# Eight unused full-array matmuls per row, and a burst of 18, in the polynomial attention of an audio tower on one core

## What is computed

```python
qn = _normalize(q) * (scale * temperature)          # 8 heads of 8 channels
kn = _normalize(k) * scale
vN = concatenate([ones, v], -1) / N                 # N = 188
kv_mod = einsum('bhni,bhnj,bhne->bhije', kn, kn, vN)
kv     = einsum('bhnd,bhne->bhde', kn, vN)
y = A * einsum('bhni,bhnj,bhije->bhne', qn, qn, kv_mod) \
    + scale**2 * Bc * einsum('bhnd,bhde->bhne', qn, kv) + scale**4 * Cc * vsum
out = (y[..., 1:] / y[..., :1]) @ Wproj.T + bproj
```

## Time and profile before

| | |
|---|---|
| median of 3 runs | 1999.03 us (1997.1 to 2000.07) |
| profiled execution | 2006.71 us, of which span 2004.9 us |
| mean granted clock of TensorE | 0.865 |
| TensorE (PE) busy | 1719.6 us, 86% of the span, 15064 matmuls |
| VectorE (DVE) busy | 1488.5 us, 74% |
| ScalarE (ACT) busy | 756.6 us, 38% |
| GpSimd (POOL) busy | 690.5 us, 34% |

### The profile page before, as it was taken

How to read it: one execution, slowest core, us unless ns; L and a number is a source line. 1 busy time by engine, 2 the same in 40 slices (tenths; PEclk the granted TensorE clock), 3 DMA queues, 4 the chain that set the end, 5 groups by cost and what they waited for, 6 DMA issues and landing times. The chain is left out here.

```text
span 2004.9 us, 45616 instructions
## 1 busy us (share of the span) xinstructions
PE 1719.6 (86%) x15064; PEld 1344.4 (67%) x15064; DVE 1488.5 (74%) x4423; ACT 756.6 (38%) x2274; POOL 690.5 (34%) x957
## 2 busy tenths in 40 slices
PE   1499999999769999999999999973999999788887
PEld 1266666666557777777777777752888888677776
DVE  6166676666627898888889888875766665688887
ACT  2245454545324444344344444321222222343442
POOL 2622222222134555545545445532211111322221
PEclk9999999999869999999999999985555555788788
DMA  2000000000000000000000000000000000000000
GB/s 114 1 2 0 0 0 0 0 0 0 1 1 1 1 2 0 0 0 0 0 0 0 0 0 0 1 1 0 1 0 0 0 0 1 1 5 8 4 6 11
DMA packets 6980, 8.13 MB, mean 4 GB/s; under 512 B 6272, under 2 KB 6272, under 8 KB 6784
## 3 DMA queue, kind: packets, MB, share of 16 engines
q1 hardware_dynamic: 6912, 7.25, 1.1%
HBM read 5.71 MB, written 1.54 MB: 4 GB/s over the span
## 5 line engine op out<-in xcount | busy, mean ns | idle before, releaser
L1142 ACT ACTIVATE ex_pT<-ex_T 128x376 f32<-128x376 f32 (+1 forms) x384 | 162.8, 440 | 217.1 <-PE ex_T L1044 207.9
L604 ACT ACTIVATE al_prob<-al_S,al_negmax 94x94 f32<-94x94 f32 (+1 forms) x512 | 146.2, 375 | 180.0 <-DVE al_negmax L731 180.0
L1207 DVE TENSOR_REDUCE ex_negmax<-ex_R 94x2 bf16<-94x376 f32 (+1 forms) x384 | 186.8, 543 | 30.6 <-PE ex_R L1015 30.0
L1044 PE MATMUL ex_T<-ex_qm,ex_kpad 128*128 128x188 f32 x1024 | 189.7, 329 | 0.0
L505 PE MATMUL al_S<-al_kpad,al_qT 128*94 128x376 f32 x384 | 166.5, 516 | 0.0
L1044 PEld LDWEIGHTS ex_T<-ex_qm,ex_kpad 128*128 128x128 f32 x1024 | 163.0, 192 | 5.1
L944 POOL TENSOR_SCALAR_AFFINE_SELECT ex_pT<-ex_pT 128x512 f32<-128x512 f32 x128 | 84.3, 659 | 236.5 <-ACT ex_pT L1142 236.5
L682 POOL TENSOR_TENSOR al_kpad<-al_kT,al_quad_mask 128x1504 f32<-128x1504 f32 x32 | 86.2, 2692 | 186.3 <-ACTq L619 186.3
L731 DVE TENSOR_REDUCE al_negmax<-al_S 94x2 f32<-94x376 f32 (+1 forms) x192 | 99.1, 542 | 62.6 <-PE al_S L506 56.7
L1554 POOL TENSOR_TENSOR ta_kk<-ta_ext 94x320 f32<-94x320 f32 x64 | 60.4, 961 | 246.4 <-DVE ta_qkn L1734 163.0
L1027 PE MATMUL ex_R<-ex_sxT,wsb 128*128 128x188 f32 x256 | 72.3, 364 | 47.5 <-DVE ex_negmax L1207 47.5
(11 more groups left out here) (308 smaller groups left out, 4300.8 us busy)
## 6 DMA issues: line engine op xcount, KB each, us to landing
tok_xin<-x_t SPq DMA_DIRECT2D x4, 760.0 KB, 6.9
wsb<-weights SPq DMA_DIRECT2D x1, 2531.0 KB, 14.2
out<-stream SPq DMA_DIRECT2D x16, 94.0 KB
tok_par<-tok_w SPq DMA_DIRECT2D x1, 4.5 KB, 1.7
```

The lines of the kernel that those rows point to most:

```text
L604: last = nc.scalar.activation(p[:, k, cols], S[0:P, k, cols], ACT.Exp, bias=negmax[g % 2][:, m:m + 1])
L1044: last = nc.tensor.matmul(T[:, k, (j % 2) * N:(j % 2 + 1) * N], kpad[par][:, j, 0:K0], qm[e % 2][:], start=True, stop=True)
L1142: nc.scalar.activation(pT[e % 2][rows, k, cols], T[rows, k, cols], ACT.Exp)\
L1207: red(dst, src, AX.X, ALU.max, negate=True).then_inc(sem["r_used"], 1)
```

## The change

TensorE gets a helper that issues matmuls whose results nobody reads: 128 rows by 128 columns of weights from `w_parts`, 512 columns of data from `w_parts`, bf16, into the bank that the next step overwrites. Per turn in which its step is valid it issues three ahead of `QQ`, one ahead of `KV`, one ahead of `Y`, two ahead of `QKV` and one ahead of `XT`, each behind that step's waits. In turn 7, before the first `OUT` transpose, it issues 18 more. One of the two `sem_inc(settled)` goes. Nothing else changes, and the other engines get the same instructions as before.

```diff
-    ident, ones = env["ident"], env["ones"]
+    ident, ones, w_parts = env["ident"], env["ones"], env["w_parts"]
+    WARM = 18
...
+            def keep_busy(bank, n):
+
+                for _ in range(n):
+                    nc.tensor.matmul(bank, w_parts[:, 0, 0:128], w_parts[:, 0, 128:640], start=True, stop=True)
+
             def body(t, par):
                 r = t - 7
+                if isinstance(r, int) and r == 0:
+                    keep_busy(OUT[:], WARM)
...
                     need(pe, qqT_ready, 3 * r)
+                    for bank in (QQ0, QQ1, QT):
+                        keep_busy(bank[:], 1)
...
                     need(pe, kv_ready, 3 * r)
-
+                    keep_busy(KV[:], 1)
...
                     need(pe, y_ready, r)
+                    keep_busy(Y[:], 1)
...
                     need(pe, qkv_ready, r)
+                    keep_busy(QKV[:], 2)
...
                     need(pe, xT_ready, r)
-                    pe.sem_inc(settled, 1)
+                    keep_busy(XT[:], 1)
```

## The result

The changed kernel takes 2006.59 us (median of 9 runs, 1999.37 to 2012.97), the kernel before 1999.03 (median of 9). The ratio is 1.0037 with a 95% interval of 1.0022 to 1.0052: slower by 7.6 us, where 47 were forecast. One execution of the kernel before, of 4323 us, that fell in the first round of experiments counts as slow and is in none of the ratios. The profiled execution took 2011.12 us, with a span of 2009.2. In the two profiled executions the layer, from its first matmul to the start of its last lot of them, went from 320.6 us (1391.90 to 1712.49) to 332.9 (1387.57 to 1720.51), so by 12.3 us. The other layers, which were not changed, came out 8 us shorter in that execution: the layer's first matmul starts 4.3 us earlier, and 3.7 us less follow behind it.

What follows compares the result with a forecast made beforehand. The prediction took TensorE at half clock to bound the attention layer. Fixed costs of 21 us plus 25.6 us over 27 full turns gave +47, less 7.7 from the profiled 2006.7: 2046 us, range 1964 to 2082.

Steps and rivals of the forecast that it cites:

- the likeliest case: Full-clock share between 0.1 and 0.35 in the 27 full turns, 2015 to 2070 us; chance 0.55.
- the break-even case: Full-clock share from 0.41 to 0.47 in the full turns, time within 4 us of 1999; chance 0.05.
- What bounds the layer: Polynomial attention: TensorE at half clock, 9.85 us a turn; VectorE's floor 7.2 us, full-clock turns 7.2 to 7.5.
- Price of an unused matmul: Each 512-column unused matmul takes 0.43 us at the half clock, 0.21 us at the full one.
- The start: Turns 1 to 6 and the burst of 18 before the full turns: +9.6 and +6.4 us.
- f = 0.2: Share of PE's working time at full clock in the 27 full turns; 10.8 us a turn, +25.6 us.
- the mixture's 0.7: Full-clock share in the mixture layer, from its mean clock of 0.85; taken as a case between the bounds.
- The formula 12.35/(1 + f) + 0.5: Length in us of a full turn with full-clock share f, not under 7.2; break-even 9.07 us at f = 0.44.
- The end: Turns 34 to 37 carry 16 unused matmuls, 6.8 us at low clock, 3.4 at full; taken as 5 us.
- The signs: Profile: 0.50 until the burst, then mean near 0.6, falls during `KV` and `Y`, rises near `QQ`; refuted above 0.72.
- Rival "the clock holds": Full clock through the layer, turns of 7.2 to 7.5 us, -50 us, 1949 us; chance 0.11.

Runs made afterwards that it cites:

- lean: As late, with one unused matmul ahead of `QKV` in place of two; 1933.6 us, ratio 0.9675 to the kernel before.
- late: As hold, but with no unused matmul ahead of turn 7 except the burst of 18; 1935.8 us, ratio 0.9699 to the kernel before.
- qq4: The changed kernel with four unused matmuls ahead of `QQ` in place of three; 1986.6 us, ratio 0.9936 to the kernel before.
- hold: The changed kernel plus unused matmuls before the `added` wait, in `KV`, and two between `Y` halves; one moved from `QQ` to `XT`; 1943.6 us.
- burst_only: The changed kernel without the eight unused matmuls per row, burst of 18 kept, second signal back; 1999.9 us, ratio 0.9996 to the kernel before.
- thin: The changed kernel with unused matmuls of 32 columns of weights in place of 128, same streamed columns; 2115.6 us, ratio 1.0578 to the kernel before.

## Why the prediction was wrong

The direction was right and the sum of +47 us was not. The wide range from 1964 to 2082 us holds the 2006.6, but the likeliest case with its own 2015 to 2070 us does not, and the measured share of full clock, 0.42, lies in the break-even case, which was given a chance of 0.05 (0.41 to 0.47) and a time within 4 us of 1999. The direction has some luck in it: more than half of the +47 was to come from the 27 turns, and these came out 1.6 us shorter; the layer is slower only by its start and its end. By the prediction's own steps:

- **What bounds the layer: right.** Half clock, PE-bound, 9.85 us a turn. At the full clock a turn is 7.41 us (lean) to 7.64 (late, with two unused matmuls in VectorE's chain), in the changed kernel 7.45, where 7.2 to 7.5 was given.
- **Price of an unused matmul: right.** 0.43 us at the half clock and 0.21 at the full one were taken; the rows have 1505.79 to 1506.22, 0.43, and 1489.32 to 1489.54, 0.22. A turn wholly at the half clock is 13.1 us, where 12.85 was the sum.
- **The start: mis-sized.** 9.6 + 6.4 = 16 us were taken. From the first `XT` to turn 7's `OUT` transpose it went from 25.6 us (1391.90 to 1417.46) to 33.3 (1387.57 to 1420.90), +7.8. The step assumed that the clock rises only in the burst; it rose in turn 6. So part of turn 6's own work ran at double speed, and the burst took 3.9 us (1417.01 to 1420.90), all of it at the full clock.
- **f = 0.2, "nearer to this layer's 0 than to the mixture's 0.7": this is the step that failed.** Measured, 0.42. It was to cost 25.6 us over 27 turns, and they came out at 264.3 us against 265.9, a gain of 1.6. The step behind it was "I expect the clock to fall there nearly every turn, and then to be short of dense work for most of a slow turn". The places of the rise and the fall were foreseen about right, how often they come was not. The same sparse stretch was passed at the full clock turn after turn, for 33 us on end, before the clock fell; and in four turns of each cycle the clock rose for a moment, so that such a turn took 10.1 us, a third of it at the full clock. A hold over several turns and a flicker in each turn were treated as rivals, and the kernel does both in alternation. The neighbours in the trace before, 0 and 0.7, did not determine where between them it would lie. What sets the length of the stretches stays open.
- **The formula 12.35/(1 + f) + 0.5: too kind.** With f = 0.42 it gives 9.2 us, measured 9.79. It credits full-clock time with PE's speed, while VectorE's 7.5 us caps it. Mixing by time the changed kernel's own turns, 13.1 us at the half clock and 7.45 at the full one, gives 1/(0.58/13.1 + 0.42/7.45) = 9.9 us, and for the break-even turn of 9.07 us a share of 0.59, where the formula had 0.44; qq4 has just these 9.07 us at 0.60. The two errors had opposite signs: by the formula f = 0.42 would have been worth 27 x (9.85 - 9.2) = 18 us of gain where 1.6 came, so the second error hid part of the first.
- **The end: right.** 5 us were taken; from turn 34's `OUT` transpose to the last it took 34.4 us (1685.21 to 1719.61) against 28.3, +6.2.
- **The signs:** the rise near `KV`, behind the `QQ` lot, was as foreseen, and the falls that are shown lie just behind `KV` and `Y`, ahead of `QKV`. "0.50 until the burst" was wrong (it rose in turn 6), the mean clock of the full turns is 0.71 and not near 0.6, which is just short of the 0.72 that was to refute the forecast, and the turns are 9.8 us on the mean, not 10 to 11.
- **Rival "the clock holds":** not what this kernel does, but reachable: 1943.6 us in hold, where 1949 was given. Its argument against was a fall behind sparse work; with more filling there, and more in sum, the falls were gone.

The layer's +12.3 us is so 7.8 - 1.6 + 6.2, but for rounding. That the medians differ by 7.6 and not by 12 us is within what one execution differs from another (1999 to 2013 us for the changed kernel); what gave some of it back in the other layers was not followed up.

## What to carry to other kernels

Where the granted clock is at half in a stretch in which TensorE is busy, ask what fills the array: 95% busy with narrow fp32 matmuls held nothing here. Unused full-width matmuls can buy the clock if there are enough of them. The readings here suggest a dense lot to raise it and filling in the sparsest stretch so that it never falls, but the kernels that held the clock also had 1.3 to 1.4 times the changed kernel's unused columns, so place is not shown apart from amount. Half a cure costs as much as it brings, since it pays in the slow turns at double price; read at which instruction the clock falls and try filling the stretch ahead of it. Put the filling into TensorE's waits and behind what the next engine waits for: 0.21 us out of the chain to `QKV` took turns from 7.64 to 7.41 us.

## What the runs showed of the hardware

- The clock can be low for 320 us under a busy engine (0.50 with PE busy 190.77 of 200 us), and once raised it was lost with PE busy 4.00 of 4 us up to 1425 (burst_only). Weights of 32 columns in place of 128, with equal streamed columns per row and more busy time, took the share of full clock from 0.42 to 0.10 (thin); yet a burst of them raised it, and it was full over the next 16.4 us.
- Rise and fall lock to the turns. Four turns of 10.1 us at a mean clock of 0.66 are followed by two of 13.1 us at 0.50 and three of 7.5 us at 1.00, with a mixed turn of 8.3 to 8.5 us on either side of the three; the cycle came twice (the windows of the changed kernel above, which cover one and the start of the next).
- More work can take less time: 32 more unused matmuls of 512 columns in qq4 were worth 20 us.
- A matmul with 32 columns of weights delayed the start of the next one of another kind by 0.14 us more than one with 128 did, at equal streamed columns and at the half clock.
